# Scale and shift of the first norm moved into ScalarE's copy of the transposed x, and the second batch's x loaded earlier, in an adaLN attention layer

## The reference

```
mod = silu(c) @ wmod                     -> sa, ca, ga, sb, cb, gb   (256 each, per batch)
ga, gb = sign * max(|.|, 0.25)
h = layernorm(x) * (1 + ca) + sa
q, k, v = h@Wq+bq, h@Wk+bk, h@Wv+bv      (16 query heads over 4 key heads, 16 wide)
y = causal softmax(rope(q) rope(k)^T / 4) v ;  heads of one group summed on the way to Wo
x = x + ga * (y @ Wo + bo)
h = layernorm(x) * (1 + cb) + sb
x = x + gb * ffn(h)
ffn: a = (rmsnorm(h) @ wv + bv) @ wo ; hh = h + a ; mlp = (silu(rms(hh)@w_gate) * (rms(hh)@w_up)) @ w_down
     where(router > 0, hh + mlp, h)
```

## Time and profile before

| what | value |
|---|---|
| median of 3 runs | 474.8 us (474.42 to 476.8) |
| the profiled execution's own time | 476.08 us |
| its span, first to last instruction | 474.4 us |
| mean granted TensorE clock | 0.984 of full |
| TensorE busy | 442.2 us |

### The profile page before, as it was taken

How to read it: one execution, slowest core, us unless ns; L and a number is a source line. 1 busy time by engine, 2 the same in 40 slices (tenths; PEclk the granted TensorE clock), 3 DMA queues, 4 the chain that set the end, 5 groups by cost and what they waited for, 6 DMA issues and landing times.

```text
span 474.4 us, 9509 instructions
## 1 busy us (share of the span) xinstructions
PE 442.2 (93%) x3336; PEld 375.7 (79%) x3336; DVE 351.2 (74%) x772; ACT 301.5 (64%) x622; POOL 228.3 (48%) x296
## 2 busy tenths in 40 slices
PE   7986889978999999999899999989999999999994
PEld 7674565866687789787659999989788799999994
DVE  4869967898984489889846888988867646678541
ACT  2387478685698867346785775457757797655440
POOL 6396538620455451214847324645542635475334
PEclk9987989999999999999999999999999999999999
DMA  6904200000010000010020000010011001001011
GB/s 188 321 9 139 92 7 1 2 0 3 0 33 0 2 1 1 31 61 1 32 78 23 2 1 2 0 47 2 0 37 46 1 0 46 3 1 46 1 46 44
DMA packets 16448, 16.04 MB, mean 34 GB/s; under 512 B 4105, under 2 KB 14798, under 8 KB 16402
## 3 DMA queue, kind: packets, MB, share of 16 engines
q1 hardware_dynamic: 16402, 15.43, 10.4%
HBM read 11.09 MB, written 4.21 MB: 32 GB/s over the span
## 4 chain that ended last, share of the span: by engine, by line
PE 73%; DVE 12%; ACT 5%; POOL 3%; issue 3%; DMA 3%; SPq 1%; POOLq 0%; DVEq 0%; ACTq 0%
PE banks L727 7%; PE banks L799 7%; PE banks L715 7%; PE banks L801 7%; PE banks L800 7%; PE banks L691 5%; PE banks L580 5%; PE banks L582 5%; PE banks L581 5%; PE banks L670 4%; DVE mxp L1180 3%; PE banks L680 2%; PE banks L782 2%; PE banks L763 1%; PE banks L656 1%
## 5 line engine op out<-in xcount | busy, mean ns | idle before, releaser
L799 PE MATMUL banks<-gTh,guhi 128*128 128x256 f32 x352 | 101.1, 287 | 1.6 <-DVE gTl L1252 0.5
L801 PE MATMUL banks<-gTh,gulo 128*128 128x256 f32 x352 | 98.7, 280 | 0.0
L800 PE MATMUL banks<-gTl,guhi 128*128 128x256 f32 x352 | 98.7, 280 | 0.0
L938 ACT ACTIVATE PT<-banks 128x1024 f32<-128x1024 f32 (+3 forms) x96 | 75.2, 811 | 30.9 <-PE banks L715 25.0
L799 PEld LDWEIGHTS banks<-gTh,guhi 128*128 128x128 f32 x352 | 66.4, 189 | 3.5 <-issue 2.4
L800 PEld LDWEIGHTS banks<-gTl,guhi 128*128 128x128 f32 x352 | 66.4, 189 | 0.4
L801 PEld LDWEIGHTS banks<-gTh,gulo 128*128 128x128 f32 x352 | 66.3, 188 | 0.0
L1180 DVE TENSOR_REDUCE mxp<-banks 128x2 f32<-128x1024 f32 (+3 forms) x56 | 61.8, 1143 | 3.7 <-PE banks L691 2.2
L691 PE MATMUL banks<-QKT 128*128 128x512 f32 (+3 forms) x192 | 52.1, 380 | 8.1 <-ACT QKT L916 5.5
L715 PE MATMUL banks<-QKT 128*128 128x512 f32 (+3 forms) x192 | 51.4, 367 | 1.7 <-DVE fft L1267 0.8
L715 PEld LDWEIGHTS banks<-QKT 128*128 128x128 f32 x192 | 30.4, 189 | 24.0 <-issue 20.8
(11 more groups left out here) (181 smaller groups left out, 1123.0 us busy)
## 6 DMA issues: line engine op xcount, KB each, us to landing
xres<-in_L_attn_x SPq DMA_DIRECT2D x8, 512.0 KB, 4.3
out_x<-xres SPq DMA_DIRECT2D x8, 512.0 KB, 3.0
wm_st<-in_L_wmod SPq DMA_DIRECT2D x1, 1024.0 KB, 9.3
modB<-mod_scratch SPq DMA_DIRECT2D x4, 256.0 KB, 3.3
wg_st<-in_L_ffn_w_gate SPq DMA_DIRECT2D x1, 704.0 KB, 5.2
wu_st<-in_L_ffn_w_up SPq DMA_DIRECT2D x1, 704.0 KB, 6.3
xres<-in_L_ffn_w_down SPq DMA_DIRECT2D x1, 640.0 KB, 6.2
wm_st<-in_L_wmod SPq DMA_DIRECT2D x1, 512.0 KB, 5.4
```

Source lines behind the costliest of these rows:

```text
L799: pe.matmul(out_, guhi[:, k, blk, :], gh, start=(m == 0 and k == 0), stop=False)
L800: pe.matmul(out_, guhi[:, k, blk, :], gl, start=False, stop=False)
L801: i = pe.matmul(out_, gulo[:, k, blk, :], gh, start=False, stop=(m == len(blocks) - 1 and k == KB - 1))
L938: act.activation(PT[:, u % 2, 2 * q:2 * q + 2, 0:CH - q0], both("prob", b, n)[:, :, 0:CH - q0], ACT.Exp, scale=float(D) ** -0.5).then_inc( ...
```

## The change: what it does

- `bias`, `biasq` and `wts` are gone, with `bias_q` and `Wq_b`. `qkv` multiplies by the plain `Wqkv`, and `qkvb` adds the plain `bqkv`.
- `xev` puts scale and shift on the transposed x: two instructions, one for each half of the features, each over both tiles of the pair, with the scale and the bias as per-partition operands. The first one waits for `modc`.
- Both chunks of batch 1's x are loaded in SP's hand-written part, ahead of the wait for the gates' modulation; in the list `ldx` acts only for b > 1.
- The six filling matmuls stand at the head of the first `qkv` (`FILL`), and `free` is taken ahead of the other waits in `qkv` and `mtT`.
- Three of GpSimd's gate instructions use another pair of operations for the same value.
- `ORDER` is a new list with the same steps, less the twelve that are gone.

```diff
-WARM, WARM2, WIDE = 14, 6, CH // (2 * KB * B)
+WARM, WIDE = 14, CH // (2 * KB * B)
+FILL = {('qkv', 0): 6}
...
 ORDER = """
-ldx ldx pzero stats asetw setw pmodc vmodc setb wts stats vkeys rstd1 norm1 norm1 xT4 norm1 norm1 xT5 xev qkv4 asetb
-bias6 biasq rstd1 xev qkv5 norm1 pmod norm1 norm1 norm1 xT7 xev amod pprep0 xT6 afwv gmod ldG ldx qkvb qkvb rope sthi
-stlo qkv7 xev pprep1 aw1 qkv3 ldB stack4 stack0 stk stk aprep qkvb qkvb rope sthi max4 aprep max0 max6 mxr mxr mxr ldW
-max2 gw1 stlo gprep gprep mxr max0 mxr aprep gprep max4 mxr stats stack6 stack2 stk max6 stk max0 max2 mxr mneg mtT4
...
+ldx ldx ldx ldx pzero stats asetw pmodc rstd1 norm1 setw norm1 vmodc xT4 xev qkv5 norm1 norm1 xT4 xev qkv4 setb stats
+pmod rstd1 norm1 norm1 xT6 asetb qkvb qkvb vkeys rope xev pprep0 amod afwv qkv6 norm1 norm1 xT7 xev pprep1 sthi qkv7
+aw1 gmod qkvb aprep stlo stack4 stack0 gw1 stk stats max4 stk rstd1 gprep qkvb rope sthi aprep norm1 norm1 gprep max6
+mxr mxr stlo max0 mxr max4 max2 mxr stack6 stk stack0 max4 max6 mxr mxr mxr max2 max4 stk max0 aprep mneg mtT6 mrow
...
+            for c in range(NC):
+                load_x(1, c)
             sp.wait_ge(s_gmod, 1)
             sp.dma_start(mod_dram, modr).then_inc(s_modw, 16)
...
-                elif kind == "ldx" and b > 0:
+                elif kind == "ldx" and b > 1:
...
-                    pool.tensor_scalar(rows[:, 2, :], rows[:, 2, :], 1.0, 0.0, ALU.add, ALU.add)
+                    pool.tensor_scalar(rows[:, 2, :], rows[:, 2, :], 1.0, 1.0, ALU.mult, ALU.add)
...
-                    then(pool.tensor_scalar(gsgn, gsgn, -1.0, 0.0, ALU.add, ALU.add))
+                    then(pool.tensor_scalar(gsgn, gsgn, 1.0, -1.0, ALU.mult, ALU.add))
...
-                    then(pool.tensor_scalar(gabs, gabs, 0.25, 0.0, ALU.max, ALU.add))
+                    then(pool.tensor_scalar(gabs, gabs, 3.0e38, 0.25, ALU.min, ALU.max))
...
+                def fill(kind, n):
+                    free(kind, n)
+                    for _ in range(FILL.get((kind, n), 0) if b == 0 else 0):
+                        pe.matmul(of(kind, b, n)[:, 0:P], ident[:], ident[:], start=True, stop=True)
...
-                elif kind == "bias":
-                    if b == 0:
-                        pe.wait_ge(s_setV, V_MODC)
-                        pe.wait_ge(s_setM, M_SETW)
-                    free(kind, n)
-                    o = of(kind, b, n)
-                    for k in range(KB):
-                        i = pe.matmul(o[:, 0:QKV], modc[:, 0, k, b:b + 1].to_broadcast([P, P]), Wqkv[:, k, :],
-                                      start=(k == 0), stop=(k == KB - 1))
-                    i.then_inc(S["bias"], 1)
...
-                    if b == 0 and n == 1:
-
-                        for _ in range(WARM2):
-                            pe.matmul(bank(7)[:, 0:P], ident[:], ident[:], start=True, stop=True)
                 elif kind == "qkv":
-                    if n == 0:
-                        wait("wts", 1)
+                    fill(kind, n)
+                    if b == 0 and n == 0:
+                        pe.wait_ge(s_setV, V_SETW)
+                        pe.wait_ge(s_setM, M_SETW)
                     wait("xev", n + 1)
-                    free(kind, n)
                     o = of(kind, b, n)
                     for t in range(2):
                         for k in range(KB):
-                            i = pe.matmul(o[:, t * QKV:(t + 1) * QKV], xTc[:, t, k, :], Wq_b[:, k, :],
+                            i = pe.matmul(o[:, t * QKV:(t + 1) * QKV], xTc[:, t, k, :], Wqkv[:, k, :],
...
-                    act.activation(xTc[:].rearrange("p t k n -> p (t k n)"), of("xT", b, n), ACT.Copy
-                                   ).then_inc(S["xev"], 1)
+
+                    if b == 0 and n == 0:
+                        act.wait_ge(s_setV, V_MODC)
+                    o = of("xT", b, n).rearrange("p (t k n) -> p t k n", t=2, k=KB)
+                    for k in range(KB):
+                        i = act.activation(xTc[:, :, k, :], o[:, :, k, :], ACT.Identity, bias=modc[:, 0, k, b:b + 1],
+                                           scale=modc[:, 1, k, b:b + 1])
+                    i.then_inc(S["xev"], 1)
...
-                elif kind == "wts":
-                    if b == 0:
-                        dve.wait_ge(s_setV, V_MODC)
-                        dve.wait_ge(s_setM, M_SETW)
-                    earlier("qkv", NJ)
-                    for k in range(KB):
-                        i = dve.tensor_scalar(Wq_b[:, k, :], Wqkv[:, k, :], modc[:, 1, k, b:b + 1], None, ALU.mult)
-                    i.then_inc(S["wts"], 1)
...
-                elif kind == "biasq":
-                    if b == 0:
-                        dve.wait_ge(s_setV, V_SETB)
-                        dve.wait_ge(s_setM, M_SETB)
-                    wait("bias", 1)
-                    dve.tensor_tensor(bias_q[:, b, :], of("bias", b, 0)[:, 0:QKV], bqkv[:], ALU.add
-                                      ).then_inc(S["biasq"], 1)
...
-                        wait("biasq", 1)
                         earlier("pv", NP)
                         if b == 0:
+                            dve.wait_ge(s_setV, V_SETB)
+                            dve.wait_ge(s_setM, M_SETB)
                             dve.wait_ge(s_const, C_ZERO)
...
                     dve.tensor_tensor(qk[:, at:at + 2].rearrange("p t h e i -> p t (h e i)"), o[:, :, 0:2 * H * D],
-                                      bias_q[:, b, 0:2 * H * D].unsqueeze(1).to_broadcast([P, 2, 2 * H * D]), ALU.add)
+                                      bqkv[:, 0:2 * H * D].unsqueeze(1).to_broadcast([P, 2, 2 * H * D]), ALU.add)
```

More of the change, by code:

```diff
@@ L67 @@
 LO_P = 1
-PE_STEPS = dict(bias=1, xT=NJ, qkv=NJ, stack=NJ, max=NM, mtT=NC, prob=2 * NP, pv=NP, yT=NC, ynT=NC, wo=NJ, hT=NJ,
+PE_STEPS = dict(xT=NJ, qkv=NJ, stack=NJ, max=NM, mtT=NC, prob=2 * NP, pv=NP, yT=NC, ynT=NC, wo=NJ, hT=NJ,
                 a=NT, h2T=NJ, gate=NJ * NG, up=NJ * NG, down=NT)
@@ L73 @@
                  sil=NJ * NG, ffhi=NJ * NG)
-DVE_STEPS = dict(wts=1, wob=1, wol=1, biasq=1, stats=NC, qkvb=NJ, rope=NC, stlo=NC, mxr=NM, mneg=NC, ytm=NC, x1=NJ,
+DVE_STEPS = dict(wob=1, wol=1, stats=NC, qkvb=NJ, rope=NC, stlo=NC, mxr=NM, mneg=NC, ytm=NC, x1=NJ,
                  norm2=NJ, hlo=NJ, route=NT, h2lo=NJ, fft=NJ * NG, fflo=NJ * (NG - 1), sum=NT)
@@ L83 @@
 SINGLE, PAIR = 1, 2
[L84 removed]
+BANKS = dict(xT=SINGLE, qkv=SINGLE, stack=PAIR, max=PAIR, mtT=SINGLE, prob=PAIR, pv=SINGLE, yT=SINGLE,
              ynT=SINGLE, wo=SINGLE, hT=SINGLE, a=SINGLE, h2T=SINGLE, gate=SINGLE, up=SINGLE, down=SINGLE)
@@ L98, in released @@
         return "ycopy", P_UNITS[n][0] + 1
-    by = dict(bias="biasq", xT="xev", qkv="qkvb", stack="stk", max="mxr", mtT="mrow", prob="exp", yT="ytm", ynT="ynev",
+    by = dict(xT="xev", qkv="qkvb", stack="stk", max="mxr", mtT="mrow", prob="exp", yT="ytm", ynT="ynev",
               wo="x1", hT="hlo", a="route", h2T="h2lo", down="sum")
@@ L112 @@
[L112 to L131, removed]
@@ L137 @@
-h2hi h2lo hmod rstd2 mrd prob0 prob2 prob6 exp exp exp a5 route wol a4 prob0 route prob2 ldG store pv5 prob6 exp prob0
-pv exp exp prob2 prob6 wts wo4 x1 exp prob0 exp ms2 ms2 pv pv exp exp prob2 qkv4 rstd2 rs2 prob0 exp exp prob2 xT7 xev
-h2 pmask pmask pv pv exp prob0 exp ldx hT6 hhi stats hlo rstd1 pmask norm1 prob2 gate7 prob0 wo6 x1 norm1 ldW wob exp
-ms1 rs1 h2 exp pmask norm1 up2 h2T1 norm2 hmod norm1 rstd2 pv pv ycopy h2hi a0 up6 route a5 h2lo qkvb qkv0 sil fft
-ffhi ms2 hT4 route ldB gate7 gate5 yT1 xT2 sil ms2 rs2 hhi ms1 xev qkvb rs1 fft rope up3 up0 h2 sil ffhi gate7 gate2
@@ new lines @@
+prob4 prob6 exp exp mneg exp mtT1 mrow pmask pmask pv pv ycopy yT0 norm1 ldx xT1 xT6 wob woh stats rstd1 norm1 xev ytm
+ynT7 ynev wol mrd prob0 prob4 exp prob2 wo7 wo0 norm1 norm1 norm1 stats exp rstd1 prob4 pv1 exp exp prob2 prob4 exp
+exp pv prob2 prob4 pv exp x1 rstd2 x1 rstd2 norm2 exp prob2 prob4 exp pv prob2 ldW wob norm2 stats hmod hT0 hmod exp
+exp prob4 qkv7 exp hhi xev ms1 prob4 prob2 pmask pv pmask pv hlo a6 exp exp prob2 prob4 rs1 a0 pmask exp exp pmask
+route rstd1 ms2 hT2 hhi ms1 route ms2 rs2 rs1 pv pv ycopy qkv6 xT0 xev xT1 yT3 qkv0 xev h2 qkvb hlo a2 h2 h2T1 h2hi
@@ new lines @@
+exp pmask rs1 fft up1 xT4 sil pv pv ycopy hT0 hhi xT5 mneg mtT6 mrow fflo ffhi fft ffhi wol hlo yT3 ytm xev fflo gate7
+sil hmod ms1 gate6 sil a2 a4 route hT3 hhi mrd hlo ynT7 ynev prob0 norm1 ffl norm1 norm1 down6 sum route ldW wob ms2
+exp prob2 exp down7 sum ms2 norm1 rs2 prob0 exp fin prob2 wo4 wo7 prob0 exp h2 pv6 pv h2 exp prob2 prob0 exp exp x1
+rstd2 x1 a4 a7 prob2 prob0 exp rs1 route ms2 pv pv exp route ms2 prob2 exp pmask rstd2 h2T7 norm2 prob0 h2hi up4 fft
+h2lo prob2 pv exp exp ffhi fflo rs2 h2 h2 prob0 prob2 exp exp qkv7 pmask pv prob0 exp xev prob2 exp pmask pmask ldB
@@ new lines @@
+rstd2 gate7 up2 fflo max4 a3 down0 sil fft fft store mxr ldx mrd x1 sum prob6 down2 ffhi ffl ffhi exp prob4 exp route
```

(4 more changed lines are left out.)

76 lines of the change are left out of this document (42 added, 34 removed).

## The result

The changed kernel takes 470.83 us (median of 7 runs, 470.13 to 472.88), the kernel before 474.94 us in the same series (7 runs, 474.36 to 476.8). The ratio is 0.9919, 95% interval 0.9904 to 0.9933: 3.9 us faster. The forecast of 471.8 us lies 1.0 us above that, and the measured time lies within its own range of 468.5 to 474.5. The profiled execution took 471.21 us for a span of 469.5 us, against 474.4 before.

What follows compares the result with a forecast made beforehand. TensorE bounds from 100 us on, VectorE's maxima from 30 to 60. Terms -2.6 (bias) + 0.9 (xev) + 0.8 (opening) - 2.1 (x) = -3.0 us: 474.8 to 471.8 us, own range 468.5 to 474.5, 8 in 10 runs 465 to 477.5.

Steps and rivals of the forecast that it cites:

- the bias term: TensorE's bias matmuls leave: batches 1, 2 and 3 give 1.3 + 0.65 + 0.65 = 2.6 us, bounds 1.3 and 3.3.
- the count of nothing: First batch's bias matmuls, between the first two `qkv`: no gain, since ScalarE's copy holds the second anyway.
- xev outside the opening: Two exposed longer copies beyond the opening, 0.43 us each, make TensorE wait: 0.9 us lost.
- the opening: First `qkv` 0.4 us earlier, second 0.5 us late, delay reaching the first `stack`: 0.8 us lost, between 0 and 1.5.
- The pair's price: ScalarE's two `xev` copies with scale and bias: 1.02 us, 0.43 us longer than the one copy before.
- rival 3: ScalarE becomes the bound, every `xev` holding TensorE or an `exp`: 477.0 us, 478.6 at the high price; chance 0.12.
- Early x: VectorE's 1.04 us load wait goes, up to 1.8 us of batch 1's statistics fill a gap: 2.1 us gained.
- The gates: GpSimd's three changed instructions save 0 to 5 us of its time, but nothing that sets the end waits: 0.
- The order is worth nothing in the sum: New step order: smallest covers between producers and consumers mostly alike, so 0, with 5 us either way in the range.
- rival 1: New order also closes half of TensorE's 10.4 us of idle time from 100 to 450 us: 466.6 us; chance 0.18.
- The signs that it named: No bias rows, `xev` pairs about 1.0 us, `stats` near 28 us, maxima 2 us sooner, middle idle near 10 us.

Runs made afterwards that it cites:

- Run 12: Kernel before with only the bias matmuls and their sums (`bias`, `biasq`) removed, leaving the shift out; 474.44 us, ratio 0.9996.
- Run 5: Kernel before with bias, biasq and wts gone and fillers moved, step list otherwise kept, xev one plain copy without scale and shift; 475.43 us, ratio 0.9993.
- run 2: Kernel before with bias, biasq and wts gone, scale and shift in xev, fillers moved; step list otherwise kept, x late, gates as before; 479.02 us, ratio 1.0059.
- run 6: Changed kernel with xev as one plain copy, scale and shift left out; 469.95 us, ratio 0.9874 to the kernel before.
- the fold: Part of the change: bias, biasq and wts away, scale and shift in xev, fillers moved; alone in the old list 479.02 us.
- run 3: Kernel before with only the early load of both chunks of batch 1's x; 472.71 us, ratio 0.9946.
- run 7: Changed kernel with batch 1's x loaded behind the write of the modulation; 480.62 us, ratio 1.0107 to the kernel before.
- run 4: Changed kernel with the three old pairs of operations in GpSimd's gates; 471.73 us, ratio 0.9925 to the kernel before.
- run 1: Changed kernel with its list put back to that of before, less the twelve removed steps; 474.25 us, ratio 0.9977 to the kernel before.

## Why the prediction came out right, and which of its steps failed

The sum was -3.0 us, and -3.9 was measured. That it came so near is luck: the bias term gave nothing of its -2.6, the longer copies cost more than was counted, and the list, counted at nothing, and a larger gain with the load made it up. By terms:

- **The bias term, -2.6 us ("those of b=1, 2 and 3 lie in a TensorE queue that is nearly full"): failed.** Run 12 measures it alone: -0.2 us (ratio 0.9996), and -1.6 at most by the interval. For batch 0 the count of nothing was right: in run 12's profile the first two `qkv` still begin 2.31 us apart, and TensorE waits 0.84 us for the copy where it waited 0.19. A stretch that is 97% busy is not one whose every instruction lies on the chain; the chain of waits did show these rows, but not that the next wait would take over the time they left. Run 5 says the same of all three removals.
- **xev outside the opening, +0.9, and the opening, +0.8: 1.7 together.** The pair's price was right (1.02 us). Runs 5 and 2 price the longer copies at 3.1 us in the old list, run 6 and the change at about 2.1 in the new one, for 1.7 in the sum. In the opening the two `qkv` moved as foretold, counted from `pmodc`'s start: 0.4 us sooner and 0.5 us later. The first `stack` is 1.3 us late, 1.7 so counted, for 0.8: what was underrated is the chain behind the second `qkv`. The third `qkv` waits 0.77 us for its copy, where it waited for none, the `xT` behind it now delays `pprep1` and the last `qkv`, and `stlo`'s long instruction adds 0.4 us. That ScalarE would become the bound (rival 3) is excluded for the new list, and was halfway true in the old one, where the fold alone costs 2.8 us. The Trainium skill, "ScalarE: Activation LUTs", section "What ACT_TABLE_LOAD costs", would make the pair 1.08 us as an estimate; the trace agrees within 6%. Its section "Rules for kernel authors" prefers VectorE for adds and multiplies; runs 2 and 5 fit that: the work put on ScalarE cost 3.1 us, and 3.6 us less on VectorE gave nothing that can be told.
- **Early x, -2.1: the size nearly right, half of the reason missing.** -2.6 alone (run 3). The wait of 1.04 us is gone, and `stats` stands at 28.7 us as foretold. In the old list `stats` stays among the maxima, so that the 1.04 us of the wait is all that the prediction would have there; the other half is `mneg`'s row, which leaves GpSimd's side (run 3), a gain that it did not have. In the new list everything hangs on it (run 7).
- **The gates, 0: right** (run 4). The write of the modulation leaves at 30.67 us in place of 33.47, and behind it SP's queue stands another 13.7 us for ScalarE's `mrow`, so nothing gains by it.
- **"The order is worth nothing in the sum": failed.** It is worth 2.7 us (run 1 against the change). It is not rival 1: the idle time from 100 to 450 us has not moved (10.1 for 10.4). About 1 us of it is the shorter toll of the longer copies (3.1 to 2.1 us, from intervals that overlap). In the opening, perhaps in part the same time, `mneg` starts at 42.04 us, and at 43.38 in run 1's timeline, 1.3 us later, where `stats` still stands between the maxima:

```profile
40.24 1.39 DVE L1104 BATCH_NORM_STATS2 st<-xres 128x6 f32<-128x256 f32 x4
43.38 0.24 DVE L1177 TENSOR_SCALAR mt<-mx 128x8 fp32r<-128x8 f32 x2
```

  The prediction had taken this move for a part of the load's 2.1; it belongs to the list. The mean granted clock also rises, from 0.991 in run 1 to 0.993. The rest is open.

By single edits, then: fold +2.8, load -2.6, gates 0, list -2.7; together -2.5, and the change gives -3.9. The remainder of 1.4 us is of the size of the intervals, or the load and the fold help each other (run 1 against run 2 is 0.992, 3.9 us for load and gates). The rows from the first `stack` to the closing reduction don't show such help: the load shortens them by 2.6 us there too (31.8 us in run 2, 29.2 in run 1). The mean granted clock does rise more, from 0.985 to 0.991, where run 3 has 0.991 for 0.988; that is not settled.

The signs that it named: no bias row; `xev` 1.02 us a pair and 16.4 us in all; `stats` at 28.74 us; the maxima of batch 0 end 3.1 us sooner (2 said), 1.2 of it by `mneg`'s row; idle of 10.1 us in the middle (10 said); `qkv` waits 2.2 us for `xev` (3 was the limit). All came true with two wrong terms in the sum: signs that only look where an event stands don't test a term like that of the bias. Only taking it out alone did.

## What to carry to other kernels

Taking work from the engine that bounds a kernel is worth only what the wait behind it doesn't take back: price it by removing it alone, not by its busy time, even in a stretch that is 97% busy. Work moved onto a copy between two matmuls is paid for at each place where the consumer stands behind it. A load that is issued earlier is worth more once the list can place the work that needs it into a gap; cost the load and the list together. And look at what the other engines do beside a short instruction once it moves: here that was worth as much as the wait.
